# Two matmul layers, the second by a nested fast scheme: half of each sum of x1's inner quadrants moves from VectorE to GpSimd

## What is computed

```python
x = x + einsum('bsi,boi->bso', x, weight[itok_B_3_7])                  # this is x1
A, Bm = lora_As[itok_B_0_23], lora_Bs[itok_B_0_23]
x = x + (einsum('bti,oi->bto', x, W) + b + (x @ A) @ Bm * 2.0)        # this is y
```

## Time and profile before

| | us |
|---|---|
| median of three runs | 2598.77 |
| the profiled execution, whole | 2599.5 |
| its span in the trace | 2597.8 |
| second stage, from its first matmul to the end | 1479.9 to 2597.8 |
| TensorE busy over the span | 2559.7 |
| VectorE busy | 1663.0 |
| GpSimd busy | 1241.5 |
| ScalarE busy | 875.9 |

### The profile page before, as it was taken

One profiled execution on the slowest core, in us unless ns is written; L12 is line 12 of the kernel. 1 busy time (PEld: TensorE's weight loads), 2 busy tenths in 40 slices (PEclk: granted clock), 3 DMA queues, 4 the chain that ended last, 5 costly groups with the idle time before them and its releaser, 6 DMA issues.

```text
span 2597.8 us, 30974 instructions
## 1 busy us (share of the span) xinstructions
PE 2559.7 (99%) x11232; PEld 2108.5 (81%) x11232; DVE 1663.0 (64%) x1880; ACT 875.9 (34%) x1157; POOL 1241.5 (48%) x1470
## 2 busy tenths in 40 slices
PE   8999999999999999999999999999999999999998
PEld 6888888888888888888888778878887788888787
DVE  5455454464463364544533577999999778999896
ACT  3232242242242232322422334333333343333332
POOL 3334434444443344334323566555666655555565
PEclk9999999999999999999999999999999999999999
DMA  9888889999998898899968885445777955444665
GB/s 353 307 297 299 297 282 282 306 298 306 287 302 281 257 314 289 280 276 264 253 196 198 262 302 190 143 144 167 235 249 239 386 166 174 166 150 121 232 228 199
DMA packets 238667, 648.03 MB, mean 249 GB/s; under 512 B 30132, under 2 KB 46516, under 8 KB 238516
## 3 DMA queue, kind: packets, MB, share of 16 engines
q0 software_dynamic: 123168, 392.24, 47.0%
q1 hardware_dynamic: 114772, 252.77, 30.1%
q10 hardware_dynamic: 576, 1.05, 0.1%
HBM read 433.07 MB, written 212.86 MB: 249 GB/s over the span
## 4 chain that ended last, share of the span: by engine, by line
PE 93%; DMA 3%; DVE 2%; issue 1%; POOL 0%; ACT 0%; SPq 0%; DVEq 0%; ACTq 0%
PE bank L814 18%; PE bank L815 18%; PE bank L816 18%; PE bank L844 12%; PE bank L848 12%; PE bank L846 12%; DMA bm<-bs 2%; PE bank L799 1%; PE bank L800 1%; DMA wl<-w1s 1%; PE bank L862 1%; DVE xc L713 1%; DVE c L778 0%; DMA xq<-xss 0%; POOL wl L397 0%
## 5 line engine op out<-in xcount | busy, mean ns | idle before, releaser
L814 PE MATMUL bank<-x_hi,w_hi 128*128 128x512 f32 x2048 | 797.6, 389 | 11.5 <-DVE x_lo L635 11.5
L397 POOL TENSOR_TENSOR wl<-wl 128x512 fp32r<-128x512 f32 x392 | 591.1, 1528 | 448.3 <-ACT wl L558 446.7
L816 PE MATMUL bank<-x_hi,w_lo 128*128 128x512 f32 x2048 | 797.4, 389 | 0.0
L815 PE MATMUL bank<-x_lo,w_hi 128*128 128x512 f32 x2048 | 797.4, 389 | 0.0
L844 PE MATMUL bank<-xc,wl 128*128 128x512 f32 x1568 | 614.3, 392 | 13.0 <-DVE xc L713 6.9
L846 PE MATMUL bank<-xc,wl 128*128 128x512 f32 x1568 | 611.3, 390 | 0.0
L848 PE MATMUL bank<-xc,wl 128*128 128x512 f32 x1568 | 611.2, 390 | 0.0
L512 ACT ACTIVATE w_hi<-w_raw 128x1024 fp32r<-128x1024 f32 x256 | 257.7, 1053 | 981.3 <-PE bank L816 974.6
L734 DVE TENSOR_TENSOR x_raw<-bank,x_raw 128x512 f32<-128x512 f32 x128 | 88.5, 691 | 695.4 <-PE bank L816 645.1
L814 PEld LDWEIGHTS bank<-x_hi,w_hi 128*128 128x128 f32 x2048 | 384.9, 188 | 91.4 <-issue 11.5
L815 PEld LDWEIGHTS bank<-x_lo,w_hi 128*128 128x128 f32 x2048 | 384.9, 188 | 79.9
(11 more groups left out here) (45 smaller groups left out, 1660.3 us busy)
## 6 DMA issues: line engine op xcount, KB each, us to landing
w_raw<-w0T SPq DMA_DIRECT2D x256, 512.0 KB, 7.9
wl<-w1s SPq DMA_DIRECT2D x392, 256.0 KB, 2.7
xss<-x_raw POOLq DMA_DIRECT2D x256, 256.0 KB, 4.4
w1s<-q_raw POOLq DMA_DIRECT2D x196, 256.0 KB, 7.3
q_raw<-w1T POOLq DMA_DIRECT2D x96, 512.0 KB, 9.6
xq<-xss POOLq DMA_DIRECT2D x40, 1024.0 KB, 7.2
x1s<-x_raw POOLq DMA_DIRECT2D x128, 256.0 KB, 2.9
c<-x1s POOLq DMA_DIRECT2D x32, 1024.0 KB, 9.7
```

Of the source, the lines that this page charges most:

```text
L397: pool.tensor_tensor(w[:, 1], w[:, 1].bitcast(F32), w[:, 0].bitcast(F32), ALU.subtract).then_inc(wl_ready, 1)
L814: pe.matmul(sums[s][:], w_hi[s][:, k, :], x_hi[:, k, :], start=(k == 0), stop=False)
L815: pe.matmul(sums[s][:], w_hi[s][:, k, :], x_lo[:, k, :], start=False, stop=False)
L816: mm = pe.matmul(sums[s][:], w_lo[s][:, k, :], x_hi[:, k, :], start=False, stop=(k == KT - 1))
```

## The change

GpSimd gets an `add_terms(s)` of its own, which makes the second half of the sum; VectorE's makes the first alone. The semaphore `term_done` becomes one for each half. GpSimd's waits for both halves of step s - 1's operand (`xc_ready`), as VectorE's second half did.

```diff
-        term_done = sem("term_done")
+        term_done = [sem(f"term_done{h}") for h in range(SPLITS)]
...
+            def add_terms(s):
+
+                if s >= SEQ or not HAS_SUM[s % INNER]:
+                    return
+                j, loads = s % INNER, (s // INNER + 1) * 16
+                ks = slice(Q // SPLITS, Q)
+                into = xq[PLACE[j]][:, ks]
+                if j == 1:
+                    pool.wait_ge(xq_loaded[1], loads)
+                    pool.wait_ge(xc_ready, s * SPLITS)
+                    pool.tensor_tensor(into, xq[1][:, ks], into, ALU.subtract).then_inc(term_done[1], 1)
+                if j in (2, 4):
+                    pool.wait_ge(xq_loaded[3], loads)
+                    pool.wait_ge(xc_ready, s * SPLITS)
+                    pool.tensor_tensor(into, xq[3][:, ks], into, ALU.subtract).then_inc(term_done[1], 1)
+                if j == 5:
+                    pool.wait_ge(xq_loaded[2], loads)
+                    pool.tensor_tensor(into, xq[2][:, ks], into, ALU.subtract).then_inc(term_done[1], 1)
...
+            add_terms(1)
             pool.wait_ge(tile_done, TILES)
...
                 if step == 3 and s >= 0:
+                    add_terms(s + 2)
...
                 if HAS_SUM[s % INNER]:
-                    act.wait_ge(term_done, xc_sums(s) * SPLITS + h + 1)
+                    act.wait_ge(term_done[h], xc_sums(s) + 1)
...
-                ks = slice(h * (Q // SPLITS), (h + 1) * (Q // SPLITS))
+                ks = slice(0, Q // SPLITS)
...
                     if m == Q - 1:
-                        for h in range(SPLITS):
-                            add_terms(s + 2, h)
+                        add_terms(s + 2)
```

More of the change, by code:

```diff
@@ L687, in sum_q, with add_terms @@
                     dve.tensor_tensor(a[1], a[1], a[0], ALU.subtract).then_inc(q_added, 1)
-            def add_terms(s, h):
+            def add_terms(s):
                 if s >= SEQ or not HAS_SUM[s % INNER]:
@@ L697, in add_terms @@
                     dve.wait_ge(xq_loaded[1], loads)
-                    dve.wait_ge(xc_ready, (s - 1) * SPLITS + h + 1)
-                    dve.tensor_tensor(into, xq[1][:, ks], into, ALU.subtract).then_inc(term_done, 1)
+                    dve.wait_ge(xc_ready, (s - 1) * SPLITS + 1)
+                    dve.tensor_tensor(into, xq[1][:, ks], into, ALU.subtract).then_inc(term_done[0], 1)
                 if j in (2, 4):
                     dve.wait_ge(xq_loaded[3], loads)
-                    dve.wait_ge(xc_ready, (s - 1) * SPLITS + h + 1)
-                    dve.tensor_tensor(into, xq[3][:, ks], into, ALU.subtract).then_inc(term_done, 1)
+                    dve.wait_ge(xc_ready, (s - 1) * SPLITS + 1)
+                    dve.tensor_tensor(into, xq[3][:, ks], into, ALU.subtract).then_inc(term_done[0], 1)
                 if j == 5:
                     dve.wait_ge(xq_loaded[2], loads)
-                    dve.tensor_tensor(into, xq[2][:, ks], into, ALU.subtract).then_inc(term_done, 1)
+                    dve.tensor_tensor(into, xq[2][:, ks], into, ALU.subtract).then_inc(term_done[0], 1)
             def xc_lo(s, h):
@@ L752, in _ @@
                             xc_lo(0, h)
-            for h in range(SPLITS):
-                add_terms(1, h)
+            add_terms(1)
             for h in range(SPLITS):
```

## The result

The changed kernel takes 2661.72 us (median of 5 runs, 2650.52 to 2665.87) against 2598.77 for the kernel before (5 runs beside it). The ratio is 1.0239, with a 95% interval of 1.0223 to 1.0254: 2.4% slower. The forecast was 2629 us, the range 2602 to 2656. The direction is as forecast; the median lies 33 us above the forecast and 6 above the range. The profiled execution took 2650.5 us, the fastest of the five, inside the range.

The account below looks back on a forecast made before the run. TensorE's matmul stream was taken as the bound. New stalls of 27.2 + 10.4 + 1.6 + 2 = 41 us, less 11 us of VectorE's gaps, gave net +30 us and a median of 2629 us; range 2602 to 2656.

Parts of the forecast that it names:

- t + 9.75: Forecast time a step's first weight tile is ready, t being VectorE's sum start; TensorE could begin 4 us later than before.
- the first kind: j = 2 in outer products 2, 3, 5 and 6, 8 steps: 2.0 to 3.8 us stall each, 3.4 taken.
- the second: Two targets, no low-rank step just before, 16 steps: 0.65 us stall each, 10.4 us together.
- after low-rank steps: j = 5 in outer products 2 to 5, 8 steps: 0.2 us stall each, 1.6 us together.
- The rest, 24 steps: Steps with one target, or j = 1 behind a low-rank step: 2 us together, for weight tiles DMA brings late.
- is granted in full in every slice: Claim that TensorE, busy 99% of the span, has its full clock throughout; no half-clock cost was forecast.
- VectorE busy some 70 us less: Sign: 56 instructions of 1.22 us each leave VectorE, some 70 us of busy time, none of it TensorE's.
- TensorE's gaps that `wl_lo` ended: Sign in the list of waits: these gaps grow from 5.7 us to some 35.
- rival B: Follow-up theory: GpSimd's extra work and hold on SBUF slow VectorE, whose additions free the banks; no chance given.
- Faster: Rival: GpSimd's sum costs near 1.3 us, some 7 us of stalls, VectorE's gaps go: 2590 us; chance 0.09.
- The two balance: Rival: new stalls of some 11 us balance the gain, time 2594 to 2604 us; chance 0.08.
- Delays feed on each other: Rival: late `xc_lo(s, 1)` delays the next sum, one more us in each of 32 steps: 2660 us; chance 0.10.

Follow-up runs that it names:

- Run 1: Changed kernel, with GpSimd's half of the sum made before `wl_lo(4 s - 1)` instead of behind it: 2622.06 us, ratio 1.0102.
- runs 3 and 4: Changed kernel, GpSimd making its half only for j = 1, 4 and 5 (2610.10 us, 1.0053), or only for j = 2 (2640.73 us, 1.0179).
- The second profile: The changed kernel profiled once more, unaltered: 2657.13 us, ratio 1.0241.
- run 5: Changed kernel, with GpSimd making the last quarter of each sum (128 x 512) in place of half: 2622.31 us, ratio 1.0111.
- run 2: Changed kernel, with ScalarE preparing `wl_hi(4 s)` before `xc_hi(s, 1)`, GpSimd's order unchanged: 2621.43 us, ratio 1.0099.
- run 7: As run 1, with GpSimd's pair of `xq` loads moved behind `wl_lo(4 s)`: 2606.57 us, ratio 1.0048.
- run 8: As run 1, with GpSimd waiting at j = 5 for `xc_lo(s, 0)` before `wl_lo(4 s + 1)`: 2617.67 us, ratio 1.0063.
- run 10: Kernel before the change, with GpSimd waiting before `wl_lo(4 s + 2)` until both `xc_lo` halves are done: 2588.04 us, ratio 0.9962.

## Why the prediction was off

**Right.** That TensorE has only 7 to 16 us to win: the gaps that `xc_lo` ended fell by 12.3 us (forecast 11). That GpSimd's subtraction takes 2.4 us: 2.40. That `wl_lo(4 s)` is ready at t + 9.75 where nothing collides (9.65 in step 30) and the stalls follow from the slack there: 27.3 us measured for 27.2 in the first kind, 9.7 for 10.4 in the second, 0.5 for 1.6 after low-rank steps. Run 1 shows that GpSimd's order is the cause, and runs 3 and 4 where the loss lies. The largest stalls are in j = 2 of outer products 2, 3, 5 and 6, with the collision as worked out for step 23.

The 27.2 is in part luck. I took 3.4 us a step as a value between no collision (2.0) and a collision (3.8). The collision came in all eight steps (GpSimd's sum took 3.4 us in each), which by the forecast's sum is 30 us; and in seven of the eight VectorE began its sums 0.4 to 2.3 us earlier in TensorE's step than before, which the forecast had not in it. The two nearly cancel.

**Wrong in size: "The rest, 24 steps: ... I allow 2 us together".** Those with one target and no low-rank step before took 14.4 us alone, from nothing to 2.7 us each. The step behind it is the sentence that in the other kinds "GpSimd goes first; what is delayed is `xc_lo`, which has room". I looked for the collision at one pair of instructions, the sum and `xc_lo(s, 0)`. VectorE's first half also meets `wl_lo(4 s - 2)`, and `wl_lo(4 s)` meets `xc_lo(s, 1)`, 0.9 us each in step 57. The slack of 0.2 us there could not take even one. A second fault is that I read the slack of the kind from step 58 alone: steps 4 and 50 had none. And of what steps 2, 50 and 51 lost, 7.8 us, collisions explain a part only.

**Wrong: the clock "is granted in full in every slice", so stalls cost their length alone.** Matmuls at half clock cost 8.4 us more than before in the profiled execution and 15.0 in the second. Even before there were 11 of them, behind one stall of 4.3 us, and no slice shows them; the starts of matmuls behind a stall do.

With these two terms, +12.4 and +8.4 us, the forecast +30 becomes +51 us, the profiled difference (2648.8 - 2597.8); all others together are right to 0.2 us, in part because small errors cancel. The median lies 11 us above the profiled execution. The second profile shows that such differences come with the number of half-clock matmuls, 6.6 us for 4.5 us of span; whether they make the whole spread of 2650 to 2666 us is open, as the slower runs were not profiled. The mean granted clock on record points the same way: 0.994 in the profiled execution, 0.991 to 0.993 in the other four, which took 5 to 15 us longer.

**"VectorE busy some 70 us less" was 48.5.** Its sums fell by 59.9 us, not 68, since the remaining halves are held more often (1.43 to 1.70 us each, by line), and `xc_lo` grew by 5.3. The last 6 us are overlap between the records of one instruction and the next, which busy time counts once: the plain sum of VectorE's durations fell by 58.6.

**The signs to look for.** "TensorE's gaps that `wl_lo` ended" was a sign that the list of waits could not give, for it names the last other signal (26.5 + 14.7 us for VectorE's additions, together 41.2, where `wl_lo` has 1.7). Whoever had read it without the timeline would have taken the forecast's mechanism for refuted, and rival B for shown. Run 1, which changes nothing about VectorE's additions and takes these gaps to 0, excludes B. "The largest, over 2 us, in j = 2" of four outer products came true for all eight steps, but three others (2, 50 and 51) stand beside them.

**The rivals.** "Faster" fell by the measured 2.4%, and run 5 speaks against it under its own condition. "The two balance" fell by its stalls, 51.9 us at the starts of steps for its 11. "Delays feed on each other" gave 2660, close to the median, but for another reason: the three kinds to which it adds a microsecond have no more stall than the forecast gave them.

## What to carry to other kernels

Where two engines exclude each other at SBUF, a moved instruction collides at every place where either engine's neighbours now meet, so the slack of each kind of step is to be read from several of its steps and set against one collision for each pair, not against the one pair that the timeline happened to show. If an engine off the path runs its instructions in a row, let it wait at a place where it has time, until the critical instruction of the other has gone; here one such wait gave 0.4% with no work moved, and moving work gave nothing. A stall of a few microseconds of TensorE can cost up to twelve matmuls at half clock on top; count these in the starts of matmuls, for slices of the page hide them.

## What the runs showed of the hardware

A VectorE subtraction with two SBUF operands (1.22 us undisturbed) can be held for a whole row of back-to-back GpSimd instructions: 5.16 us behind three (run 1), 4.58 behind four that had partly run (run 2), each time to 1.1 us after the row's end, while the GpSimd instructions kept their 1.25 us. At other times it gets in behind the first: in step 23 of the kernel before, `xc_lo(23, 0)` went in after one `wl_lo` of a row. Instructions of VectorE that were held by two or more GpSimd instructions numbered 7 before, 4 after the change, 16 in run 1, 9 in run 2, 8 in run 7, 12 in run 8 and 5 in run 10. What decides between the two is open. The Trainium skill ("SBUF — State Buffer", "Who interferes with whom") tells of exclusion for a whole instruction, by the order of issue. The trace agrees with the exclusion, and shows that a row can add up to several. With the order of issue it agrees in step 57, where `xc_lo(57, 1)` came 0.15 us ahead and went first, and not always: 10 of the 16 in run 1 were issued 0.2 to 0.8 us ahead of the row's first instruction, while GpSimd was at DMA issues, and waited for the row all the same. The DMA issues by themselves don't hold VectorE: in the kernel before, an `xc_lo` issued at 2419.15 us, during a DMA issue and 0.7 us ahead of the next `wl_lo`, took its 1.22 us.

Of stalls between 2.3 and 4.1 us some are followed by matmuls at half clock and some are not, in the same place of the program: step 16's stall was followed by none in the first profile (3.3 us) and by 7 in the second (3.1 us). The length of the stall alone does not decide it (2.5 us was followed by 7, 3.4 by none).
